# Picked weights in one product, copies inside the parameter chain, tables every seven steps, GpSimd's tables behind the sums

## What is computed

```python
x = x + einsum('bct,bcd->bdt', x, W0[ids0])            # stage 0: a 64x64 matrix per batch row, 16 to choose from
x = x + ssm(x, params1, len1)                          # stage 1: causal convolution along t, kernel K1[h, t], masked by len1
x = x + (x @ W2.T + b2 + scale[a] * (x @ A[a].T) @ B[a].T)  # stage 2: along t (1024 to 1024), with a low-rank adapter
x = x + ssm(x, params3, len3)                          # stage 3: as stage 1, kernel K3[h, t], input masked too
# K[h, t] = 2 * Re( sum_n Ct[h, n] * exp(dtA[h, n] * t) ),  dtA = A * exp(log_dt)
```

## Time and profile before

| what | us |
|---|---|
| timed runs | 1570.84, 1562.27, 1569.28 |
| median | 1569.28 |
| profiled execution, own time | 1561.47 |
| its span | 1559.4 |
| PE / PEld busy | 1490.0 / 1289.5 |
| DVE / ACT / POOL busy | 1235.8 / 744.7 / 631.5 |
| mean granted clock | 0.99 |

### The profile page before, as it was taken

One profiled execution on the slowest core, in us unless ns is written; L12 is line 12 of the kernel. 1 busy time (PEld: TensorE's weight loads), 2 busy tenths in 40 slices (PEclk: granted clock), 3 DMA queues, 4 the chain that ended last, 5 costly groups with the idle time before them and its releaser, 6 DMA issues.

```text
span 1559.4 us, 36858 instructions
## 1 busy us (share of the span) xinstructions
PE 1490.0 (96%) x14983; PEld 1289.5 (83%) x14983; DVE 1235.8 (79%) x1495; ACT 744.7 (48%) x1089; POOL 631.5 (40%) x455
## 2 busy tenths in 40 slices
PE   7878787999999999999999999999999999999998
PEld 7777675788888888888888888888888888888887
DVE  8888779777787969696969696978788787969653
ACT  4544543454444545454545454535454444545433
POOL 1211046445454545454453434343535454545040
PEclk9999999899999999999999999999999999999999
DMA  8799985749483958484848566574848583858442
GB/s 287 284 354 389 358 333 160 191 111 216 88 231 76 240 91 220 101 222 94 220 111 196 137 170 163 142 190 115 201 111 210 96 232 85 226 87 230 99 135 69
DMA packets 437847, 283.43 MB, mean 182 GB/s; under 512 B 330536, under 2 KB 377136, under 8 KB 437680
## 3 DMA queue, kind: packets, MB, share of 16 engines
q1 hardware_dynamic: 388784, 175.35, 47.6%
q10 hardware_dynamic: 48928, 106.00, 19.3%
HBM read 159.20 MB, written 73.86 MB: 149 GB/s over the span
## 4 chain that ended last, share of the span: by engine, by line
PE 76%; DVE 11%; DMA 5%; issue 4%; ACT 3%; ACTq 1%; DVEq 0%; SPq 0%
PE ps L1054 35%; PE ps L964 8%; PE ps L1154 7%; PE ps L1063 5%; PE ps L1030 5%; DMA arena<-in_x_dram 4%; PE ps L1000 4%; PE ps L1167 3%; PE ps L974 3%; PE ps L856 3%; DVE arena L2042 2%; PE ps L790 1%; DVE gbuf L2033 1%; PE ps L1017 1%; ACT arena L1541 1%
## 5 line engine op out<-in xcount | busy, mean ns | idle before, releaser
L1054 PE MATMUL ps<-arena,w2t 128*128 128x256 f16 x4608 | 523.9, 273 | 6.6 <-ACT arena L1509 5.1
L1054 PEld LDWEIGHTS ps<-arena,w2t 128*128 128x128 f16 x4608 | 451.5, 98 | 64.0 <-ACT arena L1509 5.6
L711 POOL TENSOR_TENSOR arena<-arena 128x68 f32<-128x68 f32 x31 | 27.4, 884 | 664.0 <-DVE arena L2106 395.6
L2149 DVE TENSOR_TENSOR arena<-arena 128x512 f16<-128x512 f32 x128 | 106.0, 828 | 116.9 <-ACT arena L1530 116.9
L1517 ACT ACTIVATE arena<-ps,biasx 128x256 f32<-128x256 f32 x256 | 103.4, 472 | 133.0 <-PE ps L1054 95.7
L856 PE MATMUL ps<-arena 128*128 128x128 f32 x976 | 127.7, 289 | 38.8 <-DMA arena<-in_x_dram 24.6
L1530 ACT ACTIVATE arena<-arena 128x512 f16<-128x512 f32 x128 | 80.6, 630 | 162.7 <-DVE arena L2145 161.7
L856 PEld LDWEIGHTS ps<-arena 128*128 128x128 f32 x976 | 119.8, 201 | 45.1 <-DMA arena<-in_x_dram 28.2
L2012 DVE SCALAR_TENSOR_TENSOR arena<-gbuf,arena 128x1024 f16<-128x1024 f32 x60 | 150.0, 2518 | 2.7 <-ACT arena L1450 2.7
L1154 PE MATMUL ps<-arena 128*128 128x256 f16 (+1 forms) x1536 | 137.1, 246 | 1.1
L1154 PEld LDWEIGHTS ps<-arena 128*128 128x128 f16 x1536 | 122.2, 98 | 14.5 <-DVE gbuf L2033 4.8
(11 more groups left out here) (276 smaller groups left out, 2832.1 us busy)
## 6 DMA issues: line engine op xcount, KB each, us to landing
w2t<-w_scratch ACTq DMA_DIRECT2D x96, 512.0 KB, 4.2
out_dram<-arena SPq DMA_DIRECT2D x64, 512.0 KB, 2.8
arena<-in_x_dram SPq DMA_DIRECT2D x61, 512.0 KB, 9.0
gbuf<-x_scratch SPq DMA_DIRECT2D x60, 512.0 KB, 5.4
x_scratch<-arena ACTq DMA_DIRECT2D x25, 960.0 KB, 9.2
gbuf<-w_scratch ACTq DMA_DIRECT2D x32, 512.0 KB, 4.2
arena<-krow_scratch SPq DMA_DIRECT2D x31, 512.0 KB, 9.0
x_scratch<-arena SPq DMA_DIRECT2D x7, 960.0 KB, 7.2
```

The costliest lines, as they stand in the source:

```text
L1054: mm = nc.tensor.matmul(ps[:, bank, n * HW:(n + 1) * HW], weight(p, n, part, k), xx[:, :, k], start=(fresh and n == 0 and k == 0 and q == ...
L2149: tt(x3_quarter(x3l, h0, row), x3part[slot].rearrange("p (k h b) -> p k h b", k=2, h=2), x3_quarter(x3h, h0, row), ALU.subtract).then_inc( ...
```

## The change

1. Pick: `w0n` is twice as wide and holds the matrices three times: rows 0 to 31 in the left half (the second copy meets zeros of the one-hot), rows 32 to 47 in the right half; the other parts are cleared by GpSimd and VectorE. `onehot` has the even rows' ids on partitions 0 to 31 and the odd ones' on 32 to 47. One product with 128 columns of weights gives both halves.
2. Parameter chain: six `copy_odd` stand inside it (blocks 1 to 11); `param_sines` stands in ScalarE's loop at step 2; `turn_params` moves from step 1 to 6, the adapter's lots to steps 5 and 7; x loads 8 and 9 no longer wait for `params_turned`, 10 does.
3. Tables: `chunk_at(s, offset)` places part `offset` of chunk c at step 7c + 6 + offset of 64, for c = 0 to 6.
4. Transition: `make_tables(0, 1)` waits for `t_made` 4; `left_angles` and `adv_angles` of chunk 7 move from behind the first split to behind `low_diff` and the fourth split; its last `chunk_sines` from ahead of `body(0)` to behind the first two `read_part`.

```diff
@@ sync
-                sp.dma_start(w0n[0:NID, cols], ...).then_inc(w0_loaded, 16)
+            load_w0(0, 0)
+            load_w0(1, 0)
             (ids1, ids2, len3)
+            sp.wait_ge(w0_cleared, 1)
+            load_w0(2, 1)
             sp.wait_ge(ssm_loaded, 160)
...
                 if i == 0 and l == 2 * NXIN:
+                    sp.wait_ge(lrow_loaded[LOT_A], 16)
+                if i == 0 and l == 2 * NXIN + 2:
                     sp.wait_ge(params_turned, 1)
-                    sp.wait_ge(lrow_loaded[LOT_A], 16)
@@ gpsimd
+            nc.gpsimd.memset(w0n[:, C * C:2 * C * C], 0.0).then_inc(w0_cleared, 1)
...
+                    pool.wait_ge(t_made, 4)
                     make_tables(0, 1)
@@ tensor
-                    for q in range(2):
-                        mm = matmul(ps[q * C:(q + 1) * C, dgroup, ...], src[:, 8 * dgroup + e, :], onehot[...][:, q, :])
+                    mm = nc.tensor.matmul(ps[:, dgroup, e * PAIRS:(e + 1) * PAIRS], src[:, 8 * dgroup + e, :], onehot[:, :],
+                                          start=True, stop=True)
...
-                        if step == 1:
+                        if step == 5:
+                            turn_lot(LOT_A)
+                        if step == 6:
                             turn_params()
-                        if step == 3:
-                            turn_lot(LOT_A)
-                        if step == 5:
+                        if step == 7:
                             turn_lot(LOT_B)
                     else:
-                        if step == 2:
-                            sum_k(blk - 1)
+                        c = chunk_at(STEPS // 2 * blk + step, 10)
+                        if c is not None:
+                            sum_k(c)
@@ scalar
+            act.wait_ge(pick_half_cleared, 4)
             for dgroup in range(8):
-                if dgroup == 5:
-                    (wait angles_ready, Sin, Tanh)
...
+                        if step == 2:
+                            param_sines()
...
                 for p in range(2):
                     read_part(g, p, SUM_AT[p], 0, 0, 0)
+                if early:
+                    chunk_sines(NBLK - 1, 1, 5)
+                    chunk_sines(NBLK - 1, 1, 6)
                 at_least(act, past_ready, HG * g)
                 read_part(g, 0, MIX_AT[0], 2, NQ, 2, 3)
@@ vector
             exp_exact(t[6], re, t[1], t[2], t[3])
+            copy_odd(0, 1)
             tt(t[5], ar, ar, ALU.mult).then_inc(angles_ready, 1)
...
+                    for offset, what in ((1, right_angles), (2, left_angles), (3, adv_angles), (7, combine_a)):
+                        c = chunk_at(s, offset)
+                        if c is not None:
+                            what(c, c % 2)
...
-            for n in range(4):
+            for n in range(3):
                 t_split_lo(0, n)
-                if n == 0:
-                    left_angles(NBLK - 1, 1)
-                    adv_angles(NBLK - 1, 1)
...
                 if early:
+                    t_split_lo(0, 3)
+                    left_angles(NBLK - 1, 1)
+                    adv_angles(NBLK - 1, 1)
                     combine_a(NBLK - 1, 1)
```

146 lines of the change are left out of this document (80 added, 66 removed).

## The result

The changed kernel takes 1588.2 us (median of four, 1584.28 to 1589.31), the kernel before on the same chip 1570.06 (1562.27 to 1574.17): a ratio of 1.0126, 95% interval 1.0101 to 1.0152. It is slower by some 20 us, where 1574 was forecast with a range of 1559 to 1586. The profiled execution took 1589.31 us, its span 1587.5 against 1559.4. So 28.1 us are to be found between the two traces; some 8 of them are the low profiled execution of before (1561.47 against a median of 1570).

A forecast was written before the change was run, and what follows sets the result against it. TensorE was taken to bound the kernel after about 310 us, DMA most of stage 0. Stage 0 at 0, late load +4.5 and clock +2.3 give +6.8 us: 1568.3 or 1576.1 by base, forecast 1574, range 1559 to 1586.

The forecast's parts named there:

- The pick: Opening, ahead of stage 0: 128 passes at 118 ns take 15.1 us instead of 19.1; first product at about 9.2 us.
- The bound from above: Pick: at most 19.1 us, because the same number of weight columns is loaded as before.
- Stage 0: The stage as a whole, with pick, parameters and tables: 0 us, bounds of -4 and +6.
- The chain's length: Parameter chain in stage 0: with six copies inside, it follows the products and ends at about 46 us.
- the queue would be full at the same moment within 2 us: DMA queue in stage 0: full as early as before within 2 us, first half's stores at about 53 us.
- Rival 2: Pick and late parameters delay the DMA's full stretch: stage 0 ends 4 to 6 us later, total 1581; chance 0.2.
- Tables every seven steps: Stage 0: one VectorE chunk of about 11 us moves into the DMA-bound stretch; charged 0.5 us, at most 4.
- The transition: Behind stage 0: TensorE gains 12.2 us, then waits for a late weight load; +4.5 and clock 2.3, together +6.8 us.
- first states more than 4 us from 224: Sign of being wrong, end of stage 0: the first states start more than 4 us away from 224.
- the load before 272: Sign of being wrong, behind stage 0: the weight load for slot 0 issues before 272 us.

The follow-up runs named there:

- e3: Changed kernel with each picking product of 128 weight columns split into two of 64, to lower and upper PSUM rows; 1579.2 us, ratio 1.0096 to the kernel before.
- e12: Changed kernel with w0's third copy loaded right behind the first two and the clearing limited to rows not loaded; ratio 1.0133 to the kernel before.
- e8: Kernel before with copies inside the parameter chain, late parameter transposes and tables every seven steps; old pick and transition; ratio 1.0012 to the kernel before.
- e6: Kernel before with only the tables of chunks 0 to 6 every seven steps; ratio 0.9975 to the kernel before.
- e4: Kernel before with only the edits behind stage 0 (the changed transition); ratio 1.0025 to the kernel before.
- e1: Changed kernel with the old pick (two products of 64 weight columns, w0 loaded once); 1571.9 us, ratio 1.0048 to the kernel before.
- e11: e6 with x loads 10 to 15 held until 16 blocks are summed; ratio 0.9986 to the kernel before.
- e5: e4 with chunk 7's sines and exponentials moved behind both MIX reads on ScalarE; ratio 1.0021 to the kernel before.
- e7: Kernel before with one line more: GpSimd waits for t_made before the second group's tables; ratio 0.9993 to the kernel before.
- e13: e9 with the splits of the second group's bases and tables behind load_w(7) and the third out split; ratio 0.9966 to the kernel before.
- e14: e6 with GpSimd's tables of the second group held until low_diff; 1557.6 us, ratio 0.9939 to the kernel before.
- e10: Changed kernel with each picking product split by moving columns, 32 twice, with 128 weight columns each; ratio 1.0298 to the kernel before.
- e9: e6 with GpSimd's tables of the second group held until VectorE has finished chunk 7's tables; ratio 0.9962 to the kernel before.

## Why the prediction failed, by its own steps

**The pick: the step that failed.** The prediction took 118 ns a pass and bounded the pick by 19.1 us from above, because the same number of weight columns is loaded. The pick took 28.1, 220 ns a pass. The bound from above was no bound: the 19.1 us of the earlier trace rows were those of pairs of 64 columns, of which a pair takes 148 ns, and one pass of 128 columns takes 220 (e3 against the changed kernel). The row that would have told is the earlier trace rows: stage 0's first 32 passes, with 128 weight columns, took 179 ns each. That is a mixture: the changed kernel's windows show some 200 ns a pass at 44 to 48 us (20 in 4 us) and some 105 behind 48 (38 in 4 us); passes that reach over an edge count too, so that both are a little low. The prediction set that row aside as not settled and took the 118 ns of the fast level, though the pick runs ahead of both rows. Even 179 ns times 128 is 23 us, above the bound it kept. And the first product came at 12.5 us, not 9.2: the load that was put near 9 landed at 12.0, and without that wait VectorE's masks and clearings hold it until 11.9 (e12). Of the 16.4 us that stage 0 starts later than the 25.5 of the prediction, 13.0 are the passes and 3.3 the start.

**Stage 0: put at 0, bounds -4 to +6.** It is +24.9 us in the profile. The chain's length was right: 20.5 us from stage 0's start to the parameters were predicted, 22.6 measured. What failed is the sentence that the queue would be full at the same moment within 2 us, with the first half's stores at about 53 us: the first store goes at 71.1. Of the 24.9 us, 15.4 are the start of stage 0, 1.5 the first half (29.2 us from start to store, before 27.7) and 8.0 lie behind the first store (177.8 us against 169.8). The sentence rested on the start at 25.5 us; but the step is wrong with the old pick too. In e8 stage 0 starts as before and its first states are late, and the copies in the chain with the late transposes cost 6 us by ratios. The 8.0 us come mostly with the tables: the five kernels with e6's opening take 175.4 us there on average, and up to 177.3. Rival 2 named the late stretch as the mechanism, at 4 to 6 us instead of 25.

**Tables every seven steps: charged 0.5, at most 4.** They gain 4 us (e6), against the sign of the charge: the charge for the chunk that moves into the full stretch was right in sign (the time behind the first store grows), but the gain in the opening, where the chunk was, had been left out.

**The transition: right in mechanism, half in size.** +3.2 us by the profile, 4 us by e4's ratio, +6.8 predicted. Less the shift of 24.9 us: the sums end at 250.8 (251.5 predicted), the t blocks begin at 255.1 (256.2), TensorE is through at 264.4 (265.9), the stall is released by the w_scratch load, the clock costs 2.5 us on the block behind it (2.3). Mis-sized is above all one term: the load was issued at 273.2, not 278.4, since the last angle operation ended there and not at 275.2 and the load does not wait for the sines and exponentials in front of it (3.1 us), and it landed at 276.8, not 282.6. With 276.8 and 2.5 the prediction's own sum gives +1.3, and `sum_k` does come 1.3 us later, 58.1 us behind the first states against 56.8. The other 1.9 us of the 3.2 arise behind it, where the prediction had put nothing; no run says by what.

**The sum.** 24.9 + 3.2 = 28.1 us between the profiled executions. By ratios: tables -0.25%, chain +0.37% (e8 less e6), transition +0.36% (e1 less e8; 0.25% alone), pick +0.78% (the changed kernel less e1; 0.84% alone), together +1.26%. In short, the step that failed is the price of the pick, and with it the 0 us for stage 0. The forecast's condition for being wrong, first states more than 4 us from 224, was met; the other one, the load before 272, was not. Two small readings are off and change nothing: in the earlier trace rows PEclk shows nines up to the seventh slice and its eight is in the eighth, and the sums of the four parts, 260.5 less 8.8, end at 251.7 and not 251.5.

## What to carry to other kernels

Price a product by its own shape at the clock that it will run at, and before taking "as many weight columns as before" for an upper bound ask whether the old products overlapped. In a stage that DMA bounds, ask when its first store can go: here the first states came 169 to 178 us behind it in all 17 kernels, with the first store anywhere from 49.7 to 97.9 us, while loads held back without moving it (e11) cost nothing that could be measured. Where a change moves one engine's work away from a stall, look at which other engine's work it now takes turns with; removing only the wait that ended last (e5, e7, e13) gave nothing, moving the work past the shared stretch (e14) gave 0.36% below the tables alone and 0.6% below before.

## What the runs showed of the hardware

- In the pick a pass of 128 fp32 weight columns took 220 ns with 64 moving columns and 218 with 32 (the changed kernel, e10). Two of 64 columns, to the two halves of PSUM's rows, took 148 together (e3). The next point gives the clock.
- The clock column reads 1.00 all through the opening, also where the passes are slow. In the changed kernel 20 passes of stage 0 fill 44 to 48 us, and 38 fill 48 to 52, both with 1.00; 16 fill 3.41 us at 64 to 68 with 0.50. By the passes stage 0 ran at the 1.2 GHz level up to about 48 us, and so, as its first passes follow straight on it, did the pick. So a row of the opening is to be read by its passes and not by that column.
- ScalarE's queue issued a DMA ahead of activations that stand before it, once their semaphore wait was over: the weight load went at 298.08 us beside the first sine at 298.07, though two sines, a table load of 1.28 us and two exponentials stood ahead of it. In e9 and e14 such a load and the activation before it start in the same instant, at 290.17 and at 285.71 us.
- GpSimd's small operations (128x68) ran beside VectorE's of 0.28 to 0.53 us (e14); its big ones (128x1024, 2 us and more) stretch those of 0.35 to 0.5 us to 1.9 to 2.5 us. The other way round, two small ones that take 0.3 us elsewhere took 1.27 and 1.28 us beside VectorE's splits of 1.23 (the changed kernel, from 276.90 us). The Trainium skill (SBUF — State Buffer, Who interferes with whom) has the pair of ports that the two engines share as an exclusive lock, which whoever issues first holds for the whole instruction; the rows at 288 to 295 us agree, where three VectorE operations end 0.2 to 0.3 us behind one of GpSimd's each.
